# A Mamba block with adaptive layer norm: the short convolution as diagonal matmuls, four elementwise products on GpSimd

## The reference, cut to what matters

```python
# x: (16, 512, 256); for each of the 16 sequences
xn = layernorm(layernorm(x)*(1+ca)+sa)                 # 512 x 256
def mamba(x, ...):                                    # two directions; E = 512, N = 64, K = 4 taps
    xp, z = split(x @ W_in.T)                         # 512 x E each
    xc = silu(depthwise_conv(xp, conv_w, causal) + conv_b)
    dt_lo, Bm, Cm = split(xc @ W_xp.T)
    dt = softplus(dt_lo @ W_dt.T + dt_b)
    h_t = exp(dt_t * A) * h_(t-1) + (dt_t * xc_t) * B_t    # E x N states, 512 steps
    y = (sum over N of h*C + xc*D) * silu(z)
    return y @ W_out.T
x = x + ga * (layernorm(mamba(xn) + flip(mamba(flip(xn)))) + xn)
h = layernorm(x)*(1+cb)+sb
h = silu(h @ W1 * s1) * (h @ W2 * s2)                 # 512 x 1024
h = gelu(h @ H1 * s); h = gelu(h @ H2 * s); x = x + gb * (h @ W3 * s)
```

## Time and profile before

| | us |
|---|---|
| median of 3 runs | 14339.97 (14336.53 to 14356.86) |
| the profiled execution, own time | 14347.66 |
| its span, first to last instruction | 14345.8 |
| mean granted TensorE clock | 0.81 of full |

### The profile page before, as it was taken

One profiled execution on the slowest core, in us unless ns is written; L12 is line 12 of the kernel. 1 busy time (PEld: TensorE's weight loads), 2 busy tenths in 40 slices (PEclk: granted clock), 3 DMA queues, 4 the chain that ended last, 5 costly groups with the idle time before them and its releaser, 6 DMA issues.

```text
span 14345.8 us, 177084 instructions
## 1 busy us (share of the span) xinstructions
PE 10529.0 (73%) x50188; PEld 6035.3 (42%) x50188; DVE 13278.1 (93%) x8254; ACT 10969.1 (76%) x23324; POOL 10908.2 (76%) x5124
## 2 busy tenths in 40 slices
PE   5567767777676777767777777776777767777776
PEld 2234434444343443434434344443444434344345
DVE  6999999999999999999999999999999999999992
ACT  5777777788777887778777777777777877787782
POOL 4887777787777777778777777777777777777781
PEclk7778878788787887878888788887878878788798
DMA  2223323333232332323322233232333323233232
GB/s 72 80 82 98 103 89 108 99 104 104 90 107 95 107 105 95 106 91 109 107 95 96 94 109 105 97 102 91 107 98 105 104 88 107 95 108 103 94 110 87
DMA packets 596164, 1414.30 MB, mean 99 GB/s; under 512 B 63488, under 2 KB 104592, under 8 KB 594976
## 3 DMA queue, kind: packets, MB, share of 16 engines
q1 hardware_dynamic: 595104, 1402.00, 29.9%
HBM read 1313.57 MB, written 88.18 MB: 98 GB/s over the span
## 4 chain that ended last, share of the span: by engine, by line
issue 26%; PE 26%; DVE 24%; ACT 20%; POOL 3%; DVEq 1%; DMA 0%; ACTq 0%; POOLq 0%; SPq 0%
DVE state L1196 13%; PE driven L810 7%; ACT state L985 7%; ACT v_sb L998 6%; PE q_ps L765 6%; DVE driven L1185 3%; POOL state L1226 3%; PE y_ps L824 3%; PE p_ps L681 2%; PE q_ps L752 2%; DVE xc L1156 2%; PE b_ps L800 2%; PE q_ps L775 1%; ACT L985 1%; PE p_ps L688 1%
## 5 line engine op out<-in xcount | busy, mean ns | idle before, releaser
L1226 POOL TENSOR_TENSOR state<-state,c_rep 128x1024 f32<-128x1024 f32 x4096 | 9764.5, 2406 | 3006.0 <-DVE state L1196 3005.4
L1196 DVE TENSOR_TENSOR_SCAN state<-state,driven 128x1024 f32<-128x1024 f32 x4096 | 9106.1, 2270 | 444.8 <-PE driven L810 274.1
L998 ACT ACTIVATE v_sb<-u_t,b_t 128x128 f32<-128x128 f32 x12288 | 3992.7, 505 | 2226.7 <-PE driven L810 2224.8
L985 ACT ACTIVATE state<-ud_rep,cols_sb 128x512 f32<-128x512 f32 x8192 | 5185.8, 710 | 2.4 <-PE y_ps L824 0.2
L824 PE MATMUL y_ps<-state,consts_sb 128*32 128x512 f32 x16384 | 2666.9, 729 | 2292.1 <-POOL state L1226 2289.1
L810 PE MATMUL driven<-consts_sb,v_sb 128*128 128x128 f32 x16384 | 2957.9, 344 | 1122.8 <-DVE state L1196 1113.4
L810 PEld LDWEIGHTS driven<-consts_sb,v_sb 128*128 128x128 f32 x16384 | 2432.5, 179 | 2576.9 <-DVE state L1196 2134.0
L1185 DVE TENSOR_TENSOR driven<-ud_rep,b_ps 128x1024 f32<-128x1024 f32 x2048 | 2390.2, 1213 | 16.9 <-DMA ud_rep<-ud_rows 16.9
L765 PE MATMUL q_ps<-hid,wq_sb 128*128 128x256 f32 x8192 | 2231.1, 420 | 130.0 <-ACT hid L963 83.4
L765 PEld LDWEIGHTS q_ps<-hid,wq_sb 128*128 128x128 f32 x8192 | 1596.9, 205 | 926.1 <-issue 671.7
L824 PEld LDWEIGHTS y_ps<-state,consts_sb 128*32 128x32 f32 x16384 | 347.5, 117 | 3418.0 <-POOL state L1226 3027.9
(11 more groups left out here) (113 smaller groups left out, 5202.5 us busy)
## 6 DMA issues: line engine op xcount, KB each, us to landing
c_rep<-bc_rows SPq DMA_DIRECT2D x2048, 256.0 KB, 3.0
ud_rep<-ud_rows SPq DMA_DIRECT2D x512, 512.0 KB, 3.9
wq_sb<-in_h SPq DMA_DIRECT2D x512, 512.0 KB, 3.8
wq_sb<-in_f SPq DMA_DIRECT2D x128, 512.0 KB, 4.4
wp_sb<-in_win SPq DMA_DIRECT2D x64, 512.0 KB, 3.8
ud_rows<-u_pad SPq DMA_DIRECT2D x128, 256.0 KB, 3.3
ud_rows<-dt_sb SPq DMA_DIRECT2D x128, 256.0 KB, 3.4
u_nat<-ud_rows SPq DMA_DIRECT2D x128, 256.0 KB, 3.1
```

Of the source, the lines that this page charges most:

```text
L985: ins = act.activation(state[:, unit % STATE_RING, j, :], ud_rep[:, nth % 2, j, 1, :], ACT.Exp, scale=a_neg[:, d, c, j, g:g + 1])
L998: ins = act.activation(v_sb[:, unit // 2 % V_RING, tt, :, :, n].rearrange("p j e -> p (j e)"), u_t[:, nth % 2, tt, :], ACT.Identity, scale ...
L1196: dve.tensor_tensor_scan(flat, flat, driven[:, q % DRIVE_RING].rearrange("p j t -> p (j t)"), 0.0, ALU.mult, ALU.add).then_inc(scanned, 1)
L1226: pool.tensor_tensor(part, part, c_rep[:, unit % ROW_RING, :].unsqueeze(1).to_broadcast([P, 2, T]), ALU.mult).then_inc(was_read, 1)
```

## The change

The conv becomes four matmuls for each chunk, each with a diagonal matrix of one tap as weights and a shifted view of `u_pad` as the moving side, added up in `p_ps`. They are two steps of two matmuls (K0 to K3) in the two units behind each X. ACT copies the sum with the bias to `xc` two units behind X. ACT makes the 32 diagonal matrices in the setup, they are stored to memory, and SyncE loads those of one direction (1 MB) into `dt_sb` four units ahead of each projection. The two gates (two products of 128x1024 each in place of one of 128x2048), the four `glu` products and `u` (two products of 128x1024 in two units) go to GpSimd, behind its reads of the same unit; `cut` (a small memset of VectorE) waits for the second half of `u` and comes two units later, as do the stores of u and dt. `O1` and `mix` come one unit later, and four of the eight `UT` steps (transposes of u) lie at other units.

```diff
-O1_AT, MIX_AT, N_AT = 2, 14, 24
+O1_AT, MIX_AT, N_AT = 3, 15, 24
-UT_AT = (120, 10, 25, 41, 57, 73, 89, 106)
+UT_AT = (121, 10, 26, 41, 57, 73, 78, 97)
...
-        act.append((x, part, f"X{m}", 2))
-        dve += [(x + 1 + i, part, f"conv{m}{i}", 1 + i) for i in range(2)]
+        act.append((x, part, f"X{m}", 1))
+        pe += [(x + 1 + i, part, f"K{m}", i) for i in range(2)]
+        act.append((x + 2, part, f"K{m}", 1))
...
-    dve += [(s + 19, part, "log1p", 1), (s + 19, part, "dt", 1), (s + 20, part, "u", 1), (s + 20, part, "cut", 1)]
+    dve += [(s + 19, part, "log1p", 1), (s + 19, part, "dt", 1), (s + 22, part, "cut", 1)]
+    pool = [(s + 20, part, "ua", 1), (s + 21, part, "ub", 1)]
...
-    dve.append((1, "early", "gate1", 1))
+    pool.append((1, "early", "gate1", 2))
...
-        dve += [(f_at + HC + 1 + j, part, f"glu{i}{j}", 1) for j in range(2)]
+        pool += [(f_at + HC + 1 + j, part, f"glu{i}{j}", 1) for j in range(2)]
...
-    dve.append((NG * EC + 1, "o0", "gate0", 1))
+    pool.append((NG * EC + 1, "o0", "gate0", 2))
...
+            sp.wait_ge(setup_act, 4)
+            sp.dma_start(conv_dram.rearrange("d p n -> p d n"),
+                         conv_made.rearrange("p d c k n -> p d (c k n)")).then_inc(conv_stored, 16)
             sp.wait_ge(mod_stored, 16)
+            sp.wait_ge(conv_stored, 16)
...
+            def load_conv(at, part):
+                if at.kind != "pre":
+                    wait(ud_out.sem, ud_out.before(at) if part == "p1" else ud_out.done(at, "p1", "ud"))
+                d = 1 if part == "p1" else 0
+                sp.dma_start(dt_sb[:].rearrange("p c t -> p (c t)"), conv_dram[d]).then_inc(conv_in.sem, 16)
...
+                elif name[0] == "K":                       # TensorE
+                    m = int(name[1])
+                    if quarter == 0:
+                        pe.wait_ge(act_side.sem, act_side.done(at, part, f"X{m}"))
+                        if m == 0:
+                            pe.wait_ge(conv_in.sem, conv_in.done(at, part, "conv"))
+                    for k in range(2 * quarter, 2 * quarter + 2):
+                        mm = pe.matmul(p_ps[:], conv_w[:, m, k, :], u_pad[:, m, k:k + T], start=(k == 0), stop=(k == TAPS - 1))
...
+            for d in range(2):                             # ScalarE, setup
+                for c in range(EC):
+                    for k in range(TAPS):
+                        ins = act.activation(conv_made[:, d, c, k, :], ident, ACT.Identity, scale=taps[:, d, c, k:k + 1])
...
-                        act.wait_ge(done, act_side.done(at, part, name, 0))
-                        act.activation(xc_sb[d][:, m, :], u_pad[:, m, 0:T], ACT.Identity, bias=conv_b[:, d, m:m + 1],
-                                       scale=taps[:, d, m, 0:1]).then_inc(done, 1)
+                    elif kind == "K":
+                        after_pe(pe_p)
+                        act.activation(xc_sb[d][:, m, :], p_ps[:], ACT.Identity, bias=conv_b[:, d, m:m + 1]).then_inc(done, 1)
...
+                if name in ("ua", "ub"):                   # GpSimd; gate and glu alike
+                    d, c = (1 if part == "p1" else 0), (slice(0, 2) if name == "ua" else slice(2, EC))
+                    pool.wait_ge(dve_side.sem, dve_side.done(at, part, "dt"))
+                    pool.tensor_tensor(u_sb[:, c], dt_sb[:, c], xc_sb[d][:, c], ALU.mult).then_inc(done, 1)
...
+                        dve.wait_ge(pool_side.sem, pool_side.done(at, part, "ub"))
                         emit(dve.memset(dt_sb[:, :, 0:1], NO_CARRY))
```

More of the change, by code:

```diff
@@ L602, in body @@
                         load_wdt(at, "p1")
+                    if unit == P1_AT - 4 and at.has("p1"):
+                        load_conv(at, "p1")
+                    if unit == NEXT_AT - 4 and at.has("next"):
+                        load_conv(at, "next")
                     if unit == P1_AT and at.has("p1"):
@@ L758, in network @@
                         if m == 0 and kind == "H":
-                            pe.wait_ge(dve_side.sem, dve_side.done(at, part, f"glu{i}1"))
+                            pe.wait_ge(pool_side.sem, pool_side.done(at, part, f"glu{i}1"))
                         if m == 0 and kind == "G":
@@ L1149, in step @@
                     d = 1 if part == "p1" else 0
-                    if name.startswith("conv"):
-                        m, last = int(name[4]), int(name[5])
-                        if not last:
-                            dve.wait_ge(act_side.sem, act_side.done(at, part, f"X{m}"))
-                        dst = xc_sb[d][:, m, :]
-                        for i in ((2, 3) if last else (1,)):
-                            emit(dve.scalar_tensor_tensor(dst, u_pad[:, m, i:i + T], taps[:, d, m, i:i + 1], dst,
-                                                          ALU.mult, ALU.add), i < TAPS - 1)
-                    elif name == "BC":
+                    if name == "BC":
                         dve.wait_ge(act_side.sem, act_side.done(at, part, name))
@@ L1246, in body @@
                         make_v(at, ahead)
+                    side(at, unit)
             bodies(pool, body)
```

73 lines of the change are left out of this document (43 added, 30 removed).

## The result

The changed kernel takes 13687.12 us (median of 4 runs, 13683.65 to 13708.09) against 14338.25 for the kernel before (4 runs, 14334.83 to 14356.86): the ratio is 0.9546, 95% interval 0.953 to 0.9563. The gain is 651 us, 4.5%; the forecast was 485 and its range ended at 13,700, 13 us above the time. So the direction and the order were right and the size was not.

The account below looks back on a forecast made before the run. VectorE sets the pace in most units, TensorE in some, with GpSimd nearly full in quiet pairs. Gains 462 (14 bodies at 33) + 35 + 18 - 30 = 485 us give 13855 us; 8-in-10 range 13,700 to 14,060.

Parts of the forecast that it names:

- the conv of p1: Units 16 to 26: twelve VectorE instructions leave, TensorE has room for the K steps; 79 us left, gain 15 a body.
- The pair's order: Quiet pair of units: GpSimd can be 0.4 us later, plus 0.5 idle a pair; any more stalls the scans.
- The first body, the last and the time outside the scans: Gains of 35 and 18 us for the two bodies; outside the scans ("pre", tail, setup, loads) together -30.
- VectorE's small work: Rival: thirty remaining instructions a body each wait 1.2 us more for GpSimd, 35 us, giving 14,340; chance 0.03.
- Stretch of next's conv and late glu: Units 84 to 94: from 85.47 us to 71.4, gain 14 a body; named as the riskiest part.
- My floor of 61.5: Units 84 to 94: what VectorE needs for six even and five odd units with the removed work gone.
- three stalls: Added to the floor in 84 to 94: GpSimd's late glu 3.9, TensorE beside F 1.5, beside H 4.5.
- u: Twice a body: 2.54 us leave VectorE, but `cut` waits 2.0 for GpSimd; gain 0.5 each.
- gate0: Unit 65: 2.78 us leave VectorE, GpSimd's 4.7 lie beside the next input's norm; gain 2.8.
- The early glu: Units 35, 36: 4.0 us leave VectorE, a GpSimd stall falls partly into idle time; gain 2, between 0 and 2.7.
- gate1: Unit 1, before quiet units: 2.78 us leave VectorE, GpSimd's lateness costs 3.6; gain -0.8.
- My 2 us for two-input work: VectorE's remaining two-input instructions, about thirty a body, wait more often for GpSimd: 2 us off a body.

Follow-up runs that it names:

- pool_extra: The changed kernel with GpSimd's transposed product `v_sb` made seven more times a body, in units 50 to 62: 13758.51 us, ratio 0.9593.
- k_double: The changed kernel with the first two of the four conv matmuls of each chunk run twice: 13819.46 us, ratio 0.9634.
- glu_back: The changed kernel with the four glu products of a body on VectorE again: 13763.74 us, ratio 0.9597.
- before_busy2: The kernel before with useless matmuls added, first halves of H steps made twice in units 95 and 97: 14311.62 us, ratio 0.9981.
- u_back: The changed kernel with u on VectorE in one product, cut and stores two units earlier as before: 13748.54 us, ratio 0.9589.
- glu1_at_88: All four glu products on VectorE as in `glu_back`, the late block's second two moved to unit 88: 13737.38 us, ratio 0.958.

## Why the prediction was wrong

**What held.** TensorE hides the conv of p1: 79.79 us, where I had said 79, and 14.8 gained for 15, though 2.2 are lost right behind it, by O1 and mix. The pair's order is right: GpSimd's lateness is a stall in a quiet stretch (`pool_extra`, 3.4 of 7.3 us). Beside the network more work of TensorE costs the scans (`k_double`). The first body, the last and the time outside the scans came to 41, 17.6 and -24.1 for 35, 18 and -30. The first scan is 16.9 us later, less than my 25 for "pre" and the setup; a part of the difference is that the records of X and Z last 850 ns on average up to there, 978 before the change. GpSimd's rest of VectorE's small work did not become the bound: VectorE's busy time without scans and the removed work was 13278.1 - 9106.1 - 809.9 = 3362.1 us and is 12472.7 - 9104.6 = 3368.1.

**Stretch of next's conv and late glu: 14 forecast, 18.1 measured. This is the largest error in the stretches that I costed, and it lies in the price of a late GpSimd.** My floor of 61.5 was good: VectorE is busy 61.92 us in 84 to 94, which take 66.72. On top I put three stalls side by side: GpSimd's late products 3.9, TensorE beside F 1.5, beside H 4.5, of which 1.7 were for an H that waits for the late GpSimd. The 9.9 are VectorE's idle time, and in units 84 to 94 of the changed kernel that is 4.8, by the group of its scans there; `glu_back`, where GpSimd has no late product, follows with the group of its two products:

```profile
L1214 DVE TENSOR_TENSOR_SCAN state<-state,driven 128x1024 f32<-128x1024 f32 x22 | 49.0, 2271 | 4.8 <-PE driven L843 4.8
```

```profile
L1266 DVE TENSOR_TENSOR_SCAN state<-state,driven 128x1024 f32<-128x1024 f32 x22 | 48.9, 2268 | 4.2 <-PE driven L863 4.2
...
L1164 DVE TENSOR_TENSOR hid<-hid 128x1024 f32<-128x1024 f32 x2 | 2.8, 1378 | 2.6 <-ACT hid L1025 2.6
```

TensorE alone makes the scans wait 4.2 us, near my 1.5 and 2.8. GpSimd's late products add 0.6, where I had charged 3.9 and 1.7. Taken apart by this run, the late glu's move was forecast at about -1.6 (4.0 of VectorE's work less 5.6) and is worth 4.5, and the conv's, forecast at 15.6, is worth 13.6: the error in the glu is larger than 4.1, and one in the conv hides a part of it. I read the 0.6 so: beside H TensorE is late itself, each of the two late engines catches up while the other one is waited for, and the scans pay for the longer lateness, where I had charged the sum. In the quiet stretch, where TensorE has time to spare, GpSimd's lateness was paid in full (`pool_extra`). That it is this difference between the stretches which decides is argued from the two numbers and was not tested alone. I also missed that the glu on VectorE had carried a wait for ScalarE's silu (76.5 us over 64 products, in the very row from which I took 129.4): on GpSimd the 2.6 us of it no longer stand ahead of the scans.

**Clock: 97 to 111 costed at nothing, 4.8 measured.** I had priced TensorE's clock only where the change adds work. `before_busy2` shows that a fall of the clock just ahead of a chain of sum and transposes costs 3.3 us, and that added work ahead of it, useless in itself, prevents it.

**u: 0.5 forecast, 3.4 in the first stretch.** I said that VectorE reaches `cut` 10.97 us after the last scan of unit 43 and waits 2.0 for GpSimd, in each of the 32 times. The changed kernel's rows in body 7, VectorE's and GpSimd's:

```profile
6259.62 2.33 DVE L1203 TENSOR_TENSOR driven<-ud_rep,b_ps 128x1024 f32<-128x1024 f32 x2
...
6261.96 0.06 DVE L1193 MEMSET dt_sb<- 128x4 f32 x1
```

```profile
6259.19 2.37 POOL L1264 TENSOR_TENSOR u_pad<-dt_sb,xc 128x1024 f32<-128x1024 f32 x1
```

VectorE makes the two products of the next even unit (2.33) before it comes to `cut`, at 6261.96, and GpSimd has ended at 6261.56. I had left those two instructions out of its queue. There is no wait here, and in the whole execution VectorE waits once before a `cut`, 4.9 us; `u_back` confirms the worth, 61 us.

**The small terms.** gate0: 2.8 forecast, 0.3 measured. VectorE's time does fall in unit 66, and is lost in unit 68, where the norm waits for ScalarE behind an H step that now runs at half clock (1.99 us before): the changed kernel's rows of TensorE and VectorE:

```profile
6386.46 3.78 PE L798 MATMUL q_ps<-hid,wq_sb 128*128 128x256 f32 x8
...
6393.93 0.32 DVE L1147 SCALAR_TENSOR_TENSOR small<-small 128x4 f32<-128x4 f32 x1 [3.54 <-ACT small L911]
```

The early glu was 2, between 0 and 2.7, and is at the lower end, since VectorE waits for ScalarE there in any case. gate1 I had at -0.8, and units 0 to 7 are 0.3 longer (53.59 against 53.28). O1 and mix a unit later I had not costed: +2.1 and -2.2. My 2 us for two-input work that meets GpSimd more often did not appear. That the pair's rule of the Trainium skill, "SBUF — State Buffer", "SBUF: two separate sides" (one of the two engines blocks the other for a whole instruction), holds here is seen in `glu1_at_88`, 4.84 for 2.76; but the change took such meetings away with its twelve conv instructions and added none to the rest, by the sum of 3368.1 above.

The step that failed, then, is the sum of the stalls in 84 to 94, in which a late GpSimd stood with 3.9 and 1.7 us beside TensorE's and measured 0.6, and the clock left out behind it, put at nothing and measured at 3.3 of 4.8: 4.1 + 4.8 of the 10 us a body. Too low as well were u, by 2.9 and in its second stretch by 0.9, and the 2 us of blocked instructions, which did not come; gate0 and the early glu, too high by 4.6, hid a part of this, which is luck.

## What to carry to other kernels

Where several engines are late for the same scan, do not add their lateness without looking: beside a late TensorE a late GpSimd cost 0.6 us in place of 5.6, in a quiet stretch it was paid in full. Check the sum against the idle time in the trace. Before costing an instruction that moves to another engine, read its idle time beside its busy time: a wait that leaves the critical queue may be worth as much as the instruction. And price TensorE's clock in every stretch where a chain through TensorE ends a wait, also in those that the change does not touch.
